# A software loop on TensorE's queue that runs 21 turns, the last one cut short by a branch on the loop's counter

## The reference

```python
x = x + _L0_conv_ref(_gn(x), weight, bias)            # whitening of 16 groups of 4 channels
x = x + _L1_conv_ref(_gn(x), bn_..., qk_w, v_w)       # attention in windows
```

## Time and profile before

| | us |
|---|---|
| median of 3 runs | 478.49 |
| lowest and highest | 478.12, 480.04 |
| the profiled execution, its own time | 477.33 |
| its span, from the first to the last instruction | 475.6 |
| PE busy | 433.4 |
| DVE, ACT, POOL busy | 340.8, 295.2, 192.2 |

### The profile page before, as it was taken

The page is one execution under the profiler, slowest core; times in us unless marked ns, Lnnn a source line. Parts: engine busy times, 40 slices in busy tenths (PEclk is TensorE's granted clock), DMA queues, the critical chain, the costliest instruction groups (busy, mean ns, idle before and its releaser), DMA issues. The chain is left out here.

```text
span 475.6 us, 38537 instructions
## 1 busy us (share of the span) xinstructions
PE 433.4 (91%) x17450; PEld 347.4 (73%) x17450; DVE 340.8 (72%) x1075; ACT 295.2 (62%) x518; POOL 192.2 (40%) x158
## 2 busy tenths in 40 slices
PE   7999913898778999999999999999999999999973
PEld 7899813433567887888788878887888788878862
DVE  1565378877456787778777877787778777877764
ACT  3232300477756777777777777777777777777750
POOL 4072000020133554455446544554455446544412
PEclk9999975999999999999999999999999999999997
DMA  8990000000111424334241424424142433524233
GB/s 302 419 372 5 3 0 1 1 35 35 63 52 65 144 87 144 99 112 150 79 136 76 152 86 127 130 99 144 68 145 85 144 99 113 150 80 135 77 98 71
DMA packets 31567, 52.08 MB, mean 110 GB/s; under 512 B 6176, under 2 KB 21024, under 8 KB 30624
## 3 DMA queue, kind: packets, MB, share of 16 engines
q1 hardware_dynamic: 31520, 51.50, 32.1%
HBM read 12.95 MB, written 12.85 MB: 54 GB/s over the span
## 5 line engine op out<-in xcount | busy, mean ns | idle before, releaser
L331 POOL TENSOR_TENSOR X<-X,otok 128x392 f32<-128x392 f32 x63 | 108.1, 1716 | 167.2 <-DVE otok L734 167.2
L701 DVE TENSOR_REDUCE rmax<-ps 113x16 bf16<-113x784 f32 x128 | 124.7, 974 | 58.6 <-PE ps L874 57.5
L390 ACT ACTIVATE vst<-ps 49x256 f32<-49x256 f32 x256 | 96.8, 378 | 54.8 <-PE ps L858 52.5
L909 PE MATMUL ps<-diag,qk_all 64*49 64x98 f32 x4096 | 129.5, 246 | 0.5 <-ACT prob_all L374 0.5
L909 PEld LDWEIGHTS ps<-diag,qk_all 64*49 64x49 f32 x4096 | 105.3, 120 | 31.0 <-issue 30.5
L921 PE MATMUL ps<-mdiag,sel 64*49 64x98 bf16 x2048 | 112.5, 202 | 0.3 <-DVE mdiag L709 0.2
L374 ACT ACTIVATE prob_all<-ps 113x784 f32<-113x784 f32 x128 | 105.5, 824 | 9.8 <-PE ps L921 5.7
L325 POOL TENSOR_SCALAR xs<-X,affined 128x392 f32<-128x392 f32 x64 | 68.8, 1076 | 87.5 <-DVE affined L687 59.5
L381 ACT ACTIVATE qk_all<-ps 128x784 f32<-128x784 f32 x64 | 52.7, 824 | 29.9 <-PE ps L836 29.7
L921 PEld LDWEIGHTS ps<-mdiag,sel 64*49 64x49 bf16 x2048 | 67.7, 99 | 0.6 <-issue 0.6
L957 PE MATMUL ps<-prob_all,vst 113*32 113x49 f32 x4096 | 59.2, 208 | 5.0 <-issue 5.0
(11 more groups left out here) (163 smaller groups left out, 363.7 us busy)
## 6 DMA issues: line engine op xcount, KB each, us to landing
diag<-qk_all SPq DMA_DIRECT2D x256, 98.0 KB
out<-X SPq DMA_DIRECT2D x30, 392.0 KB
X<-x_in SPq DMA_DIRECT2D x7, 1024.0 KB, 16.4
X<-x_in SPq DMA_DIRECT2D x7, 544.0 KB, 17.1
X<-x_in SPq DMA_DIRECT2D x4, 256.0 KB, 3.7
out<-X SPq DMA_DIRECT2D x2, 294.0 KB
X<-x_in SPq DMA_DIRECT2D x2, 192.0 KB, 4.7
out<-X SPq DMA_DIRECT2D x2, 98.0 KB
```

Of the source, the lines that this page charges most:

```text
L331: g.tensor_tensor(rows_of(u), rows_of(u), otok[u % 2][:].rearrange("p k a s -> p k s a"), ALU.add).then_inc(S["x_ready"], 1)
L390: ins = a.activation(vst[u % 3][64 * e:64 * e + POS].rearrange("p g k (x h) j e d -> p (g k x) h j e d", h=2)[:, :, half, :, e], ps[64 * h ...
L701: v.tensor_reduce(rmax[u % 3][0:ROW, :, 8 * k:8 * k + 8], ps[0:ROW, B_S:B_S + 2, 0:8 * POS].rearrange("p h (v q) -> p h v q", q=POS), AX.X ...
L909: ins = mm(ps[64 * e:64 * e + POS, B_ST + hh, col:col + 2 * POS], qk[u % 3][r, g, k, 2 + x_, :], diag[u % 3][r, e::2, g, k, x_, :], start= ...
```

## The change

PE's loop has 21 turns in place of 20. The third round and its projection stand under a branch on the loop's counter, which leaves them out in the last turn. So the rounds 1 to 62 run in the loop, and only the rounds 63 and 64 are written out behind it. The loop's body does the same in every turn, so three things are added to keep the counts right. The projections behind the rounds 61 and 62, of units 64 and 65 that do not exist, are executed on what lies in `xs`, and nothing reads their results. POOL gives two counts of `xs_ready` for them, once the projection of unit 63 is through (`qk_ps`). SP gives one count of `qk_kept` more, once the values of unit 62 are projected (`v_ps`), for the `project_v` of unit 63, which now waits for `qk_kept` like the others. That `project_v` and the last `weigh_values` lose their waits for `v_ready`.

```diff
--- before.py
+++ after.py
@@ -268,6 +268,9 @@
             sp.wait_ge(S["zeros_ready"], 3)
             for u in range(UNITS):
                 spread(u)
+                if u == UNITS - 1:
+                    sp.wait_ge(S["v_ps"], u)
+                    sp.sem_inc(S["qk_kept"], 1)
                 if u >= NW - 1 and u % QI == QI - 1:
                     sp.wait_ge(S["x_ready"], u + 1 - QI)
                     store((u - QI) // QI)
@@ -334,6 +337,9 @@
             for i in range(-3, UNITS + 1):
                 if has(i + 3):
                     normalise(i + 3)
+                elif i + 3 == UNITS:
+                    pool.wait_ge(S["qk_ps"], UNITS)
+                    pool.sem_inc(S["xs_ready"], 2)
                 if has(i - 2) and i - 2 < UNITS - 1:
                     add(i - 2)
 
@@ -845,10 +851,8 @@
 
                 if u == 0:
                     pe.wait_ge(S["qk_head"], 2)
-                elif u < UNITS - 1:
+                else:
                     pe.wait_ge(S["qk_kept"], 1)
-                else:
-                    pe.wait_ge(S["v_ready"], 1)
                 for k in range(KH):
                     for x_ in range(2):
                         for half in range(2):
@@ -857,7 +861,7 @@
                                 col = (2 * k + x_) * 64
                                 ins = mm(ps[64 * half:64 * half + POS, B_QKV + g, col:col + 64],
                                          xs[u % 3][r, k, 2 * x_ + half, :], wv[r, :], start=True, stop=True)
-                                if 0 < u < UNITS - 1 and (k, x_, half, g) == (0, 0, 0, 0):
+                                if u > 0 and (k, x_, half, g) == (0, 0, 0, 0):
                                     ins.then_inc(S["qk_kept"], -1)
                 ins.then_inc(S["v_ps"], 1)
 
@@ -944,8 +948,6 @@
 
                 if u >= UNITS - 2:
                     pe.wait_ge(S["o_ready"], u + CREDIT["o_ready"])
-                if u == UNITS - 1:
-                    pe.wait_ge(S["v_ready"], 1)
                 for k in range(KH):
                     for a_ in range(SUB):
                         for g in range(G):
@@ -1024,11 +1026,15 @@
             project_qk(2)
             rest(0)
             project_qk(3)
-            with pe.Fori(0, 20):
-                for r in range(3):
-                    rest(1 + r)
-                    project_qk(4 + r)
-            for i in range(61, UNITS + 1):
+            with pe.Fori(0, 21) as turn:
+                rest(1)
+                project_qk(4)
+                rest(2)
+                project_qk(5)
+                with pe.If(turn < 20):
+                    rest(3)
+                    project_qk(6)
+            for i in range(63, UNITS + 1):
                 rest(i)
```

## The result

The changed kernel takes 474.2 us in the median of 4 runs (473.63 to 474.97), the kernel before 478.89 in 4 runs of the same session (478.12 to 480.04): a ratio of 0.9900, with a 95% interval of 0.9878 to 0.9922. That is 4.7 us, twice the forecast 2.4, and 0.2 us under the forecast's range. The profiled execution took 474.15 us, its span is 472.4; against the profiled execution of before, 477.33 and 475.6, that is 3.2 us.

A forecast was written before the change was run, and what follows sets the result against it. PE bounds the loop at 5.28 us a unit; behind it, instruction-block fetches do. Gains of 2.05, 0.40 and 0.57 less 0.45 give 2.57, less 0.2 for the branch 2.4: 476.1 us on the median, range 474.4 to 478.4.

The forecast's parts named there:

- Rounds 61 and 62 move into the loop: PE behind the old loop: three instruction-fetch stalls go, two unused projections are bought, so round 63 starts 2.05 us earlier.
- Round 63: PE's round 63: 0.40 us less waiting for DVE's mask, and a 0.57 us stall in sum_weights goes.
- A new stall: PE at the 53rd matmul of round 63's weigh_values: a wait for an instruction block, 0.45 us against the gain.
- The second one: A second stall, 127 matmuls after the new one, would lie beyond the new tail, so round 64's 1.02 us goes.
- The hand-over of counts: Changed waits and counts on SP, POOL and PE: claimed to cost nothing while other waits cover them.
- Rival 3: The jump over the third round loses the loaded blocks, PE waits for fetches: 481.8 us, slower; chance 0.08.
- The branch: Loop branch on PE, 20 times not taken and once taken: 0.2 us cost in all, range 0 to 0.4.
- What of it reaches the end: Program's end: follows POOL's last addition, 2.57 us earlier, less 0.2, so 2.4 us; DVE's 3.59 is not followed.
- rival 1: The last image's queued second store overlaps the first, so the end comes 3.4 us earlier: 475.1 us; chance 0.20.
- the term of the stores: Last image's stores behind POOL's last addition: transfer time assumed unchanged, so no gain was counted there.

The follow-up runs named there:

- no_unused: Changed kernel with further branches skipping the two unused projections, and two waits for kept values back: 476.67 us, ratio 0.9931 to the kernel before.
- branch_alone: Kernel before, with only a never-skipping branch on the loop counter around the third round of its 20 turns: ratio 1.0004 to the kernel before.
- branch_three: Kernel before, with a never-skipping branch around each of the loop's three rounds, 60 executed: ratio 0.9977 to the kernel before.
- stores_three: Changed kernel with the last image stored in three parts (half, a quarter, a quarter): 474.51 us, ratio 0.9911 to the kernel before.
- store_late: Kernel before, with the store of the image before the last waiting for one more unit's addition: ratio 0.9983 to the kernel before.
- before_p3: Kernel before, unchanged, profiled once more: span 478.1 us, tail 27.04 us, with a 1.63 us wait for diag transfers in round 62.

## Why the prediction was wrong

**What held.** The mechanism held on PE. *Rounds 61 and 62 move into the loop*: round 63 was forecast 2.05 us earlier, measured 1.96 (2.02 if the 0.06 is taken off by which the last common projection was later). But the reason given for its size doesn't add up: stalls of 0.41, 0.98 and 1.08 less 1.48 are 0.99, not 2.05. The unused projections cost next to nothing (no_unused), as a round without one takes 5.29 us too; the two rounds took 12.61 us before (449.09 to 461.70) and 10.58 now. *Round 63*: the mask's 0.40 and the stall's 0.57 both went; L925 comes 0.18 us into the round, and the second scores 2.08 us into it, forecast 2.07. That this fits so well is in part luck. PE's timeline of before has the sums of round 63 at

```profile
463.08 0.78 PE L939 MATMUL ps<-prob_all,ones 113*32 113x98 f32 x25
```

so they and their stall lasted 1.66 us, to 464.74, against 1.08 now (460.74 to 461.82) and 0.82 in a loop's round: the stall cost 0.84 and not the 0.57 of its bracket, and 0.26 came back as the wait for ACT, for which there was no term. *A new stall*: forecast at the 53rd matmul of weigh_values, found behind the 54th, and sized rightly. Its bracket is 0.16 (0.29 to 0.57 in the other three profiles), but a bracket counts from the modelled end of the matmul before; weigh_values lasts 1.33 us (462.83 to 464.16) in place of 0.90, so 0.43 more, forecast 0.45. The second one, forecast to lie behind the program's last matmul, didn't come; two packets of q8, as said. *The hand-over of counts* cost nothing: no bracket of PE names a semaphore of it. Rival 3 is out: the jump forward brought no packet. The rule of the Trainium skill behind it ("Runtime: NRT & Kernel Launch", "Instruction fetch mechanics") doesn't hold for PE here; what that section states of size, 128 KiB or 2048 instructions for PE, agrees with a loop of some 1520 that stays.

**What was mis-sized in the sum.** *The branch* was put at 0.2 and costs nothing (branch_alone, branch_three). *What of it reaches the end* went wrong most: "the transfers behind it do not follow" was half true. POOL's addition came 2.51 us earlier (forecast 2.57), and DVE's 4.13 (forecast 3.59), but the stores behind POOL's then took 5.88 us and not 6.57. Of these 0.7 us, 0.48 are the second transfer of the first store, 1.25 us in place of 1.73, whose issue on SP no longer met a block for PE. So the blocks cost not only PE's time. That the second store was queued sooner isn't needed for it: in stores_three a second transfer is faster too, with nothing queued behind. It isn't the overlap of rival 1 either: the second store's packets begin 0.4 us ahead of the first one's end, and 0.3 before. Why a transfer is slower behind a long issue stays open. Together, 2.4 with 0.2 and 0.7 more and 0.06 less becomes 3.2, which is the difference of the two profiles.

**The step that failed.** Two steps of "What of it reaches the end" failed, and they make up the 1.9 us between 476.1 and 474.2. One is the term of the stores that was put at nothing: 0.7 us, with the branch 0.8. The other, 1.1 us, is its last sentence, "on the median it gives 476.1": the saving of one profiled execution was taken off the median, as if the changed kernel's profiled execution, too, lay 1.16 us below its median. It lies 0.05 us below it, 474.15 against 474.2. The first profile of before was a short one: its span is 1.32 us under the mean of its six, of which 0.96 lies ahead of the mark and 0.36 in the tail. Ahead of the mark three of the six have the lower clock in the mixing stage, 1.0 us each, and the first turn takes 32.0 to 34.1 us. The tail of the kernel before has two lengths: 26.1 to 26.3 us in three of six profiles, the first among them, and 27.0 to 27.1 in the other three, where round 62 waits longer, twice for unit 63's diag transfers and once for its block. The changed kernel has no such wait in four profiles, 23.0 to 23.4 of tail. Means of 26.63 and 23.21 make the change worth 3.4 us behind the mark, 0.2 more than the first two profiles show.

**What stays open.** Over all sessions 96 runs of the kernel before have a median of 479.3 and 19 of the changed one 474.5, so 4.8 us. The profiles' marks differ by 0.45 us in the mean (450.29 of six, 449.84 of four), in favour of the changed kernel, which with the tail makes 3.9. Ahead of the mark both kernels have the same scatter, 16.5 or 17.5 us to the first projection and 32.0 to 34.1 for the first turn, of which ten profiles are too few to say whether the last 0.9 us is more than chance. Part of the 0.45 is chance: the lower clock in the mixing stage came in three of the six and in one of the four, which is 0.25 us of the means. That a block's packet holds unit 63's transfers, and that SP's issues are long beside one, is read from the packets of 18 profiles and from where the fetches lie in them; an experiment with one fetch alone moved was not made.

The version with the stores in three parts ends 0.6 to 1.4 us sooner behind the mark than the changed kernel, but over 12 runs its median, 474.3, can't be told from that kernel's 474.5.

## What to carry to other kernels

Code that runs once behind a loop is paid at the speed at which its blocks arrive, and if rounds there resemble the loop's, a turn cut short by a branch can run them from what is already loaded, even with work that nobody needs, which here only filled a wait. Put the branch behind long matmuls, where it is free, and not behind short ones, where it opened a gap of 0.12 us. Blocks on their way also hold other transfers, so look for their packets when a DMA or its issue is late. And before a saving read from one profile is taken off a median, profile the old kernel more than once: one execution can lie over a microsecond from the middle, and waits that only half of the executions have are part of what a change removes.

## What the runs showed of the hardware that was not expected

- A block of instructions for PE took 3.4 to 4.5 us from one restart to the next in the loop's first turn too, so the first turn costs 32.0 to 34.1 us between units 2 and 7 where five later periods take 26.4.
- A block for PE is one packet, which took 0.95 us of a DMA engine in store_late and 1.52 in before_p3, and the last packets of a transfer between two places in SBUF started only when it ended. So PE waited 1.0 to 1.8 us for a spread in 5 of the 10 profiles that fetch blocks there, and in none of the 8 that don't.
- SP's issue of a transfer, otherwise 0.5 to 0.6 us, took 1.2 to 1.9 us where such a packet was in flight beside unit 63's spread, and 1.6 to 1.7 at the first store, whose second transfer then took 1.7 us in place of 1.2.
